# Weights times values of a grouped attention: two calls of four key tiles a head in place of four calls of two

## The chip, the cores and the metric

The kernel runs on one core of one Trainium2 chip. The metric is the device time of one execution in microseconds, and the comparison is between medians of several executions. The core's engines work side by side, each through its own list of instructions, and wait for each other through semaphores: TensorE (PE in the profile, its weight loads PEld), VectorE (DVE), ScalarE (ACT), GpSimd (POOL) and SyncE (SP). TensorE's clock has two levels, 2.4 GHz (granted clock 1.00) and 1.2 GHz (0.50).

## The reference

Two decoder layers over 1024 rows of 128 features: a selective scan, cross-attention, experts, causal attention, a cross-attention with state-space filter and feed-forward, and at the end a block of grouped attention and experts. Only the grouped attention matters here:

```python
NQ, NKV, HD = 16, 4, 8          # query heads, key/value heads, features of a head
q, k, v = ...                   # normalised and rotated, S rows each
k = jnp.repeat(k, NQ // NKV, axis=2)
v = jnp.repeat(v, NQ // NKV, axis=2)
scores = jnp.einsum('bthd,bshd->bhts', q, k) / np.sqrt(HD)
scores = jnp.where(causal[None, None], scores, -jnp.inf)
attn = jax.nn.softmax(scores, axis=-1)
out = jnp.einsum('bhts,bshd->bthd', attn, v)
```

## The kernel before

The program is a chain of parts with barriers between them; the grouped attention, `gqa_attend`, stands near its end, and `gqa_output` follows it. The kernel holds 1024 rows, so a head has NT = 8 query tiles and 8 key tiles of 128 (P); HALF is 512 rows. Queries and keys are split into three bfloat16 parts each.

For every one of the HQ = 16 heads five things are done:

- *Turn of the queries* (`turn`, L2623): eight transposes on TensorE, then ScalarE copies them out (qT, L2742).
- *Maxima* (L2638, L2641 on TensorE, L2722 on VectorE): for each query tile the scores of all keys up to the diagonal, with the causal mask added by a matmul, and the negated maximum of each row. Score banks are used in turn, so tile n needs that the maximum of tile n - 2 has been read.
- *Turn of the shifts* (L2623 again, 75 rows): VectorE splits the maxima into three parts (L2728 to L2731), TensorE transposes queries and maxima together, ScalarE copies them out (sT, L2752).
- *Exponentials* (L2651, L2654 on TensorE, L2759 on ScalarE): for key tile k the scores come out the other way round, keys in rows, with the maximum already subtracted; the exponential is written in float32 to `prob`. A key tile has one or two pieces of up to 512 columns, and a piece needs that the piece two before it has been read.
- *Weights times values* (`outputs`, L2670): the probabilities of a key tile times its values, 9 columns (8 features and a one for the sum). These matmuls use only a strip of 32 of TensorE's 128 columns, given by `tile_position`: even and odd key tiles and the two halves of the query rows have a strip each, four in all. All go to PSUM bank 7. A call works on a pair of key tiles: (0,1) and (2,3) have four matmuls each, (4,5) and (6,7) two, since their columns lie in the second half alone.

The order on each engine is written out by one loop over steps. Step 8h + i has the maxima of head h, tile i; the exponentials run 11 steps behind (EXP_LAG), the outputs 13 (OUT_LAG), the turn of the shifts 10 steps behind the head's first step, and the turn of the next head's queries comes at i = 5. So TensorE works on three heads at a time, and the calls of `outputs` for pairs (0,1), (2,3), (4,5), (6,7) stand at the ends of the steps with i = 6, 0, 2 and 4. When a head's last pair is done, VectorE copies and adds the two parts of its output (L2716, L2717) into `stack`, which `gqa_output` reads.

Of the kernel before, what the change touches and what calls it, by code (L numbers as in the profile page):

```python
# [23 lines left out]
P = 128  # L24
S = 1024
D = 128
NT = S // P
S2 = 6404
DC = 96
HALF = 512  # L30
# [90 lines left out]
def mamba(nc, g, t, m):  # L121
# [65 lines left out]
    N_LOADS = 13  # L187
    STEPS = NC * NS
    DT0 = BC3
# [2175 lines left out]
HQ, HKV, HD = 16, 4, 8  # L2365
# [199 lines left out]
def gqa_attend(nc, g, t, m, a):  # L2565
# [12 lines left out]
    prob = m.sb("prob", [P, 2, NT, S])  # L2578
# [26 lines left out]
    def out_quadrant(k, half):  # L2605
        q = 32 * (2 * (k % 2) + half)
        return ps[q:q + OUT, 7, :]
# [6 lines left out]

    Q_TURN, S_TURN, EXP_LAG, OUT_LAG = 5, NT + 2, NT + 3, NT + 5
    STEPS = HQ * NT + OUT_LAG

    with nc.Block() as block:
        @block.tensor
        def _(pe):  # L2620
            def turn(head, rows, done, bank=turned_bank):
                for i in range(NT):
                    last = pe.transpose(bank[0:rows, i * P:(i + 1) * P], split[:, i, head, 0:rows],  # L2623
                                        ident[:])
                last.then_inc(done, 1)

            def maxima(h, i):

                n = NT * h + i
                b = 2 * (n % 2)  # L2630
                if i == 0:
                    pe.wait_ge(q_ready, h + 1)
                if n >= 2:
                    pe.wait_ge(max_read, n - 1)
                width = (i + 1) * P
                for k in range(0, width, HALF):
                    w = min(HALF, width - k)
                    pe.matmul(ps[:, b + k // HALF, 0:w], qT[0:PARTS9, h % 2, i * P:(i + 1) * P],  # L2638
                              kT[0:PARTS9, h // (HQ // HKV), k:k + w], start=True, stop=k + w < width)
                col = (i % 4) * P  # L2640
                pe.matmul(ps[:, b + i // 4, col:col + P], ident[:], above[:], start=False,  # L2641
                          stop=True).then_inc(score_done, 1)

            def exponentials(h, k):

                if k == 0:
                    pe.wait_ge(s_ready, h + 1)
                for n, q, w in pieces(h, k):
                    if n >= 2:
                        pe.wait_ge(prob_ready, n - 1)  # L2650
                    last = pe.matmul(ps[:, 4 + n % 2, 0:w], kT[:, h // (HQ // HKV), k * P:(k + 1) * P],  # L2651
                                     sT[:, h % 2, k * P + q:k * P + q + w], start=True, stop=q > 0)
                    if q == 0:
                        last = pe.matmul(ps[:, 4 + n % 2, 0:P], ident[:], below[:], start=False, stop=True)  # L2654
                    last.then_inc(prob_psum, 1)

            def outputs(h, k):


                pe.wait_ge(prob_ready, pieces(h, k + 1)[-1][0] + 1)  # L2660
                if k == 0:
                    if h == 0:
                        pe.wait_ge(out_zeroed, 1)
                    else:
                        pe.wait_ge(o_ready, h)
                for half in range(2):
                    for kk in (k, k + 1):
                        lo, hi = max(kk * P, half * HALF), (half + 1) * HALF
                        if lo < hi:
                            last = pe.matmul(out_quadrant(kk, half)[:, lo - half * HALF:HALF],  # L2670
                                             a["v"][:, kk, h // (HQ // HKV), :],
                                             prob[:, h % 2, kk, lo - kk * P:hi - kk * P],
                                             start=kk < 2, stop=hi - (kk + 1) * P < 2 * P,
                                             tile_position=(0, 32 * (2 * (kk % 2) + half)))
                if k == NT - 2:
                    last.then_inc(pv_done, 1)

            for k in range(HKV):
                if k >= 2:
                    pe.wait_ge(k_ready, k - 1)  # L2680
                turn(HQ + k, SPLIT, k_psum, key_bank(k))
            pe.wait_ge(k_ready, HKV)
            turn(0, PARTS9, q_psum)
            for step in range(STEPS):
                h, k = divmod(step, NT)
                if k == Q_TURN and h + 1 < HQ:

                    pe.wait_ge(q_ready, 1) if h == 0 else pe.wait_ge(s_ready, h)
                    turn(h + 1, PARTS9, q_psum)
                h, k = divmod(step - S_TURN, NT)  # L2690
                if k == 0 and 0 <= h < HQ:
                    pe.wait_ge(q_ready, min(h + 2, HQ))
                    pe.wait_ge(shift_ready, h + 1)
                    turn(h, SPLIT, s_psum)
                h, k = divmod(step, NT)
                if h < HQ:
                    maxima(h, k)
                h, k = divmod(step - EXP_LAG, NT)
                if 0 <= h < HQ:
                    exponentials(h, k)  # L2700
                h, k = divmod(step - OUT_LAG, NT)
                if 0 <= h < HQ and k % 2:
                    outputs(h, k - 1)

        @block.vector
        def _(dve):
            link = chained(dve, chain_dve)
            dve.wait_ge(k_ready, HKV)
            dve.memset(ps[:, 7, :], 0.0).then_inc(out_zeroed, 1)
            for step in range(STEPS + 1):  # L2710
                h, k = divmod(step - OUT_LAG - NT, NT)
                if k == 0 and 0 <= h < HQ:

                    dve.wait_ge(pv_done, h + 1)
                    rows = a["stack"][64 * (h % 2):64 * (h % 2) + 64, h // 2, :]
                    link(dve.tensor_copy(rows, out_rows(0)))  # L2716
                    dve.tensor_tensor(rows, rows, out_rows(1), ALU.add).then_inc(o_ready, 1)  # L2717
                h, i = divmod(step, NT)
                if h < HQ:
                    b = h % 2  # L2720
                    dve.wait_ge(score_done, step + 1)
                    dve.tensor_reduce(low[:, b, i:i + 1], pair(2 * (step % 2), (i + 1) * P), AX, ALU.max,  # L2722
                                      negate=True).then_inc(max_read, 1)
                    if i == NT - 1:

                        dve.wait_ge(max_read, NT * (h + 1))
                        parts = split[:, :, h, PARTS9:SPLIT]
                        link(dve.tensor_copy(parts[:, :, 0], low[:, b, :]))  # L2728
                        link(dve.tensor_tensor(rest[:, b, :], low[:, b, :], parts[:, :, 0], ALU.subtract))
                        link(dve.tensor_copy(parts[:, :, 1], rest[:, b, :]))  # L2730
                        dve.tensor_tensor(parts[:, :, 2], rest[:, b, :], parts[:, :, 1],  # L2731
                                          ALU.subtract).then_inc(shift_ready, 1)

        @block.scalar
        def _(act):
            for k in range(HKV):
                act.wait_ge(k_psum, k + 1)
                act.activation(kT[:, k, :], key_bank(k), ACT.Copy).then_inc(k_ready, 1)

            def copy_queries(h):  # L2740
                act.wait_ge(q_psum, h + 1)
                act.activation(qT[0:PARTS9, h % 2, :], turned_bank[0:PARTS9, :], ACT.Copy).then_inc(q_ready, 1)  # L2742

            copy_queries(0)
            for step in range(STEPS):
                h, k = divmod(step, NT)
                if k == Q_TURN and h + 1 < HQ:
                    copy_queries(h + 1)
                h, k = divmod(step - S_TURN, NT)
                if k == 0 and 0 <= h < HQ:  # L2750
                    act.wait_ge(s_psum, h + 1)
                    act.activation(sT[:, h % 2, :], turned_bank, ACT.Copy).then_inc(s_ready, 1)  # L2752
                h, k = divmod(step - EXP_LAG, NT)
                if 0 <= h < HQ:
                    if h >= 2 and k == 0:
                        act.wait_ge(pv_done, h - 1)
                    for n, q, w in pieces(h, k):
                        act.wait_ge(prob_psum, n + 1)
                        act.activation(prob[:, h % 2, k, q:q + w], ps[:, 4 + n % 2, 0:w], ACT.Exp,  # L2759
                                       scale=SCALE).then_inc(prob_ready, 1)  # L2760
# [394 lines left out]
```

## Time and profile before

| | |
|---|---|
| median of 3 executions | 1744.25 us (1743.5 to 1744.35) |
| the profiled execution | 1739.54 us, its span 1737.8 us |
| TensorE (PE) busy | 1420.6 us, 82% |
| VectorE (DVE) busy | 1288.2 us, 74% |
| ScalarE (ACT) busy | 930.5 us, 54% |
| GpSimd (POOL) busy | 697.0 us, 40% |
| one head of the attention | 11.19 us |

The span is the time from the first instruction of the program to the last in the profile. Busy times are sums over all parts; what bounds one part has to be read in that part. The rows further down are of one profiled execution. A row that stands for several instructions in a run says so with "xN"; its time is from the start of the first to the end of the last. A float32 matmul leaves two records. The bracket behind a row is idle time of that engine and what ended it, as inferred from semaphores.

### The profile page before, as it was taken

The page shows a single profiled execution, that of the slowest core. Times are in us where ns is not written, and L with a number is a line of the kernel's source. Part 1 is how long each engine was busy: PE and PEld are TensorE (multiplying, and loading weights), DVE is VectorE, ACT ScalarE, POOL GpSimd, SP SyncE. Part 2 cuts the span into 40 slices and gives each one's busy share as a digit, 9 for nine tenths or more (in the row PEclk, how much of TensorE's full clock was granted, in tenths as well). Part 3 has the DMA queues.
Part 4 walks back from the last instruction along what each step waited for, and adds up shares of the span by engine and source line. Part 5 has one row for each costly group of instructions (what it writes and reads, how often), then busy time and mean ns, then how long its engine had stood idle before and what let it go on. Part 6 is the DMA issues. An engine that isn't in the chain of part 4 may idle for free. (4 is left out here: it accounts for less than half of the span.)

```text
span 1737.8 us, 19863 instructions
## 1 busy us (share of the span) xinstructions
PE 1420.6 (82%) x6581; PEld 752.1 (43%) x6637; DVE 1288.2 (74%) x3067; ACT 930.5 (54%) x1452; POOL 697.0 (40%) x529
## 2 busy tenths in 40 slices
PE   5777899899986747889898888988859339999798
PEld 2233344345544421355454554545547223333365
DVE  4998677855427539999999999999857666777433
ACT  4665212556521310788888888888831225666321
POOL 0664312012000000698898988989930030000012
PEclk9899899999987867999999999999888758999999
DMA  6000110000009320000000000000011030000000
GB/s 145 1 1 0 39 61 29 0 1 0 0 19 198 68 64 1 1 1 1 1 1 1 1 1 1 1 1 1 1 27 71 22 80 1 1 1 1 1 1 12
DMA packets 30968, 37.36 MB, mean 21 GB/s; under 512 B 13889, under 2 KB 24096, under 8 KB 29732
## 3 DMA queue, kind: packets, MB, share of 16 engines
q1 hardware_dynamic: 29312, 24.19, 5.1%
q10 hardware_dynamic: 1544, 11.79, 3.3%
q8 instruction: 56, 0.92, 0.2%
q14 instruction: 56, 0.46, 0.1%
HBM read 29.73 MB, written 6.24 MB: 21 GB/s over the span
## 5 line engine op out<-in xcount | busy, mean ns | idle before, releaser
L1461 PE MATMUL psum<-film_ka,film_context_qa 97*128 97x512 bf16 (+1 forms) x832 | 326.0, 393 | 86.8 <-DVE search_and_weigh_e L1695 36.5
L1665 DVE MAX8 search_and_weigh_kept<-psum 128x8 f32<-128x171 f32 (+2 forms) x1216 | 330.1, 324 | 0.2
L1463 PE MATMUL psum<-film_kb,film_context_qb 128*128 128x512 bf16 (+1 forms) x777 | 302.0, 390 | 0.0
L1847 ACT ACTIVATE search_and_weigh_e<-psum,search_and_weigh_bias 128x512 f32<-128x512 f32 (+1 forms) x416 | 267.5, 665 | 58.0 <-PE psum L1463 54.7
L1695 DVE SCALAR_TENSOR_TENSOR search_and_weigh_e<-psum,film_context_top,search_and_weigh_e 128x512 f32<-128x512 f32 (+1 forms) x283 | 200.0, 714 | 15.5 <-ACT search_and_weigh_e L1847 14.0
L1718 POOL TENSOR_TENSOR search_and_weigh_e<-search_and_weigh_e,search_and_weigh_keep 128x512 f32<-128x512 f32 (+1 forms) x133 | 150.6, 1132 | 108.6 <-ACT search_and_weigh_keep L1826 105.3
L1461 PEld LDWEIGHTS psum<-film_ka,film_context_qa 97*128 97x128 bf16 x832 | 86.3, 104 | 229.8 <-DVE search_and_weigh_e L1695 95.5
L1722 POOL TENSOR_TENSOR search_and_weigh_mean<-search_and_weigh_e 128x512 f32<-128x512 f32 (+1 forms) x104 | 133.4, 1283 | 11.5 <-DVE search_and_weigh_e L1695 4.4
L1752 PEld LDWEIGHTS psum<-ctx_rows,search_and_weigh_mean_T 128*128 128x128 f32 (+1 forms) x816 | 124.1, 195 | 31.3 <-issue 5.2
L2959 POOL TENSOR_TENSOR residual<-residual,top_expert_kept 128x1024 f32<-128x1024 f32 x7 | 16.5, 2355 | 292.2 <-DVE top_expert_kept L2916 292.2
L1727 POOL TENSOR_TENSOR search_and_weigh_mean<-search_and_weigh_mean,search_and_weigh_e 128x512 f32<-128x512 f32 (+1 forms) x104 | 127.9, 1230 | 8.2
L2722 DVE TENSOR_REDUCE gqa_attend_low<-psum 128x1 f32<-128x128 f32 (+7 forms) x128 | 94.0, 754 | 43.2 <-PE psum L2641 40.7
L1752 PE MATMUL psum<-ctx_rows,search_and_weigh_mean_T 128*128 128x96 f32 (+1 forms) x816 | 121.0, 271 | 1.0
L1726 POOL TENSOR_TENSOR search_and_weigh_e<-search_and_weigh_e 128x512 f32<-128x512 f32 (+1 forms) x91 | 111.8, 1229 | 7.1
L2759 ACT ACTIVATE gqa_attend_prob<-psum 128x512 f32<-128x512 f32 x192 | 84.9, 486 | 49.6 <-PE psum L2654 48.9
L1039 ACT ACTIVATE cross_attention_prob<-psum 128x1024 f32<-128x1024 f32 (+1 forms) x51 | 51.8, 1019 | 97.1 <-PE psum L998 96.4
L340 POOL TENSOR_TENSOR mamba_drive<-mamba_relu,mamba_b_all 128x1024 f32<-128x1024 f32 x32 | 77.2, 2414 | 64.7 <-ACT mamba_b_all L465 33.6
L985 PE MATMUL psum<-cross_attention_prob,ctx_rows 128*97 128x512 f32 (+1 forms) x204 | 98.2, 604 | 4.6 <-ACT cross_attention_prob L1039 4.6
L1825 ACT ACTIVATE search_and_weigh_keep<-search_and_weigh_e,search_and_weigh_below 128x512 bf16<-128x512 f32 (+1 forms) x133 | 93.5, 703 | 12.7 <-POOL search_and_weigh_mean L1727 12.2
L998 PE MATMUL psum<-oss_attention_qc_shifted,ctx_T 97*128 97x512 f32 (+1 forms) x204 | 99.3, 610 | 0.8 <-ACT oss_attention_qc_shifted L1030 0.8
L1463 PEld LDWEIGHTS psum<-film_kb,film_context_qb 128*128 128x128 bf16 x832 | 84.5, 102 | 33.4 <-issue 6.0
L1739 PE MATMUL psum<-ident,search_and_weigh_mean 128*128 128x128 f32 (+1 forms) x408 | 81.3, 281 | 11.7 <-ACT search_and_weigh_mean_T L1804 9.3
(544 smaller groups left out, 2660.1 us busy)
## 6 DMA issues: line engine op xcount, KB each, us to landing
film_kb<-film_k_rows ACTq DMA_DIRECT2D x4, 1601.0 KB
film_ka<-film_k_rows ACTq DMA_DIRECT2D x3, 1601.0 KB
ctx_T<-in_ctx_T SPq DMA_DIRECT2D x1, 2401.5 KB
gqa_experts_w<-in_L_ffn_W SPq DMA_DIRECT2D x1, 2048.0 KB
film_convolve_back<-in_dft_back SPq DMA_DIRECT2D x1, 1728.0 KB, 11.9
film_k_rows<-cross_attention_film_hi SPq DMA_DIRECT2D x6, 256.0 KB, 2.0
film_k_rows<-cross_attention_film_mid SPq DMA_DIRECT2D x6, 256.0 KB, 2.0
film_k_rows<-cross_attention_film_low SPq DMA_DIRECT2D x6, 256.0 KB, 2.0
```

Source lines behind the costliest of these rows:

```text
L985: last = pe.matmul(ps[0:CA, 6 + n, :], ctx[0:rows, k, :], prob[0:rows, k % 3, n * HALF:(n + 1) * HALF], start=k == 0, stop=k == KT - 1)
L998: last = pe.matmul(ps[0:rows, 2 * (k % 2) + n, :], ctx_T[:, k * P:k * P + rows], qc_shifted[:, n * HALF:(n + 1) * HALF], start=True, stop= ...
L1461: pe.matmul(out, a["qa"][0:ROWS, h, rows], a["ka"][0:ROWS, h, c + b:c + b + cols], start=True, stop=False)
L1463: last = pe.matmul(out, a["qb"][:, h, rows], a["kb"][:, h, c + b:c + b + cols], start=False, stop=True)
L1665: last = dve.max(kept[:, h % 2, first + s, :], bank[:, lo:hi])
L1695: dve.scalar_tensor_tensor(out=w, in0=weigh_bank(n, h), scalar=a["top"][:, NH * i + h, TOP - 1:TOP], in1=w, op0=ALU.is_ge, op1=ALU.mult).t ...
L1718: link(pool.tensor_tensor(w[h], w[h], keep[:, k % KEEPS, 0:width], ALU.mult))
L1722: link(pool.tensor_tensor(out, w[0], w[1], ALU.add))
L1726: link(pool.tensor_tensor(w[2], w[2], w[3], ALU.add))
L1727: pool.tensor_tensor(out, out, w[2], ALU.add).then_inc(mean_ready, 1)
L1752: last = pe.matmul(ps[:, 7, 0:DC], mean_T[0:r, n % 2, b:b + P], ctx[0:r, (c + b) // P, 0:DC], start=c + b == 0, stop=c + b + r == S2)
L1847: act.activation(e[:, n % RING, sub, 0:PIECES[u][1]], ps[:, SEARCH_BANKS + q % WEIGH_BANKS, 0:PIECES[u][1]], ACT.Exp, bias=bias[:, i % 2, ...
```

## The change

`outputs` works on four key tiles in a call (BURST = 4), and is called at every fourth key tile in place of every second. In a call the pairs follow each other in the order of before. It waits for the exponentials of its last key tile.

```diff
     STEPS = HQ * NT + OUT_LAG
+    BURST = 4
...
-                pe.wait_ge(prob_ready, pieces(h, k + 1)[-1][0] + 1)
+                pe.wait_ge(prob_ready, pieces(h, k + BURST - 1)[-1][0] + 1)
...
-                for half in range(2):
-                    for kk in (k, k + 1):
-                        lo, hi = max(kk * P, half * HALF), (half + 1) * HALF
-                        if lo < hi:
-                            last = pe.matmul(out_quadrant(kk, half)[:, lo - half * HALF:HALF],
...
-                if k == NT - 2:
+                for even in range(k, k + BURST, 2):
+                    for half in range(2):
+                        for kk in (even, even + 1):
+                            lo, hi = max(kk * P, half * HALF), (half + 1) * HALF
+                            if lo < hi:
+                                last = pe.matmul(out_quadrant(kk, half)[:, lo - half * HALF:HALF],
...
+                if k == NT - BURST:
                     last.then_inc(pv_done, 1)
...
-                if 0 <= h < HQ and k % 2:
-                    outputs(h, k - 1)
+                if 0 <= h < HQ and k % BURST == BURST - 1:
+                    outputs(h, k - BURST + 1)
```

The changed kernel's lines are numbered one higher from the maxima on (L2639 is the L2638 of before) and two higher in `outputs` (L2672 is L2670). A row names the line, the output and operands and the size of the result.

TensorE around exponentials 3 of a head, before: the call for pair (0,1) stands between the exponentials of key tile 3 and the next maxima.

```order
L2651 MATMUL psum<-gqa_attend_sT,gqa_attend_kT 128x512
L2654 MATMUL psum<-gqa_below,gqa_ident 128x128
L2651 MATMUL psum<-gqa_attend_sT,gqa_attend_kT 128x128
L2670 MATMUL psum<-gqa_attend_prob,gqa_v 9x512
L2670 MATMUL psum<-gqa_attend_prob,gqa_v 9x384
L2670 MATMUL psum<-gqa_attend_prob,gqa_v 9x512 x2
L2638 MATMUL psum<-gqa_attend_kT,gqa_attend_qT 128x512 x2
L2641 MATMUL psum<-gqa_above,gqa_ident 128x128
L2651 MATMUL psum<-gqa_attend_sT,gqa_attend_kT 128x512
L2654 MATMUL psum<-gqa_below,gqa_ident 128x128
```

The same place on TensorE in the changed kernel, from the last piece of exponentials 3 on:

```order
L2652 MATMUL psum<-gqa_attend_sT,gqa_attend_kT 128x128
L2639 MATMUL psum<-gqa_attend_kT,gqa_attend_qT 128x512 x2
L2642 MATMUL psum<-gqa_above,gqa_ident 128x128
L2652 MATMUL psum<-gqa_attend_sT,gqa_attend_kT 128x512
L2655 MATMUL psum<-gqa_below,gqa_ident 128x128
L2639 MATMUL psum<-gqa_attend_kT,gqa_attend_qT 128x128
L2642 MATMUL psum<-gqa_above,gqa_ident 128x128
L2652 MATMUL psum<-gqa_attend_sT,gqa_attend_kT 128x384
L2655 MATMUL psum<-gqa_below,gqa_ident 128x128
L2672 MATMUL psum<-gqa_attend_prob,gqa_v 9x512
L2672 MATMUL psum<-gqa_attend_prob,gqa_v 9x384
L2672 MATMUL psum<-gqa_attend_prob,gqa_v 9x512 x2
```

The pair (0,1) has moved behind the exponentials of key tiles 4 and 5, where it stands directly ahead of pair (2,3).

TensorE after the turn of the shifts, before: the call for pair (4,5) stands between exponentials 7 of one head and the maxima that precede exponentials 0 of the next.

```order
L2651 MATMUL psum<-gqa_attend_sT,gqa_attend_kT 128x128
L2654 MATMUL psum<-gqa_below,gqa_ident 128x128
L2670 MATMUL psum<-gqa_attend_prob,gqa_v 9x512
L2670 MATMUL psum<-gqa_attend_prob,gqa_v 9x384
L2638 MATMUL psum<-gqa_attend_kT,gqa_attend_qT 128x512
L2641 MATMUL psum<-gqa_above,gqa_ident 128x128
L2651 MATMUL psum<-gqa_attend_sT,gqa_attend_kT 128x512
L2654 MATMUL psum<-gqa_below,gqa_ident 128x128
```

The same place on TensorE in the changed kernel:

```order
L2652 MATMUL psum<-gqa_attend_sT,gqa_attend_kT 128x128
L2655 MATMUL psum<-gqa_below,gqa_ident 128x128
L2639 MATMUL psum<-gqa_attend_kT,gqa_attend_qT 128x512
L2642 MATMUL psum<-gqa_above,gqa_ident 128x128
L2652 MATMUL psum<-gqa_attend_sT,gqa_attend_kT 128x512
L2655 MATMUL psum<-gqa_below,gqa_ident 128x128
```

The pair (4,5) is gone from here, and stands directly ahead of pair (6,7), four steps after the merged call for tiles 0 to 3.

## Rows read from the trace of the kernel before

**Rows 1.** windows of one head and of the last stretch at low clock: busy us (xcount), granted clock

```profile
1491.15:1502.34 11.19, 10.31 (x82) 4.32 (x80) 7.87 (x15) 7.14 (x15) 0.00 (x0) 1.00 0.01 1
1446.00:1449.00 3.00, 3.00 (x15) 0.81 (x13) 1.52 (x2) 1.64 (x4) 0.00 (x0) 0.50 0.00 0
```

**Rows 2.** VectorE's second add for each head, L2717, of the whole trace

```profile
L2717 DVE TENSOR_TENSOR gqa_experts_stack<-gqa_experts_stack,psum x16: 689/691/693, 1457.6 to 1619.2; 64x512 f32<-64x512 f32 x16
```

**Rows 3.** waits of the attention: who waited, for whom, us, times, longest

```profile
PEld psum L2638 <- DVE gqa_attend_low L2722: 35.9, 42, 0.9
```

**Rows 4.** timeline of one head: start us, us, what, idle before and its releaser

```profile
1491.91 1.96 DVE L2722 TENSOR_REDUCE gqa_attend_low<-psum 128x1 f32<-128x768 f32 x2
...
1493.01 1.04 PE L2670 MATMUL psum<-gqa_attend_prob,gqa_v 128*9 128x512 f32 x8
1493.06 0.77 ACT L2759 ACTIVATE gqa_attend_prob<-psum 128x512 f32<-128x512 f32 x2 [0.27 <-PE psum L2654]
...
1493.99 0.61 PE L2638 MATMUL psum<-gqa_attend_kT,gqa_attend_qT 72*128 72x512 bf16 x2
...
1494.49 0.38 PE L2651 MATMUL psum<-gqa_attend_sT,gqa_attend_kT 75*128 75x512 bf16 x1
...
1495.05 0.22 PE L2654 MATMUL psum<-gqa_below,gqa_ident 128*128 128x128 bf16 x1
...
1495.20 1.05 PE L2670 MATMUL psum<-gqa_attend_prob,gqa_v 128*9 128x256 f32 x8
...
1496.18 0.28 PE L2638 MATMUL psum<-gqa_attend_kT,gqa_attend_qT 72*128 72x256 bf16 x1
...
1496.47 0.22 PE L2654 MATMUL psum<-gqa_below,gqa_ident 128*128 128x128 bf16 x1
...
1496.94 0.61 PE L2623 MATMUL psum<-gqa_ident,gqa_split 128*75 128x128 bf16 x8 [0.25 <-DVE gqa_split L2731]
...
1497.59 1.02 ACT L2752 ACTIVATE gqa_attend_sT<-psum 75x1024 bf16<-75x1024 bf16 x1 [0.48 <-PE psum L2623]
...
1497.82 1.02 PE L2670 MATMUL psum<-gqa_attend_prob,gqa_v 128*9 128x512 f32 x4
...
1498.78 0.39 PE L2638 MATMUL psum<-gqa_attend_kT,gqa_attend_qT 72*128 72x512 bf16 x1
...
1499.07 0.38 PE L2651 MATMUL psum<-gqa_attend_sT,gqa_attend_kT 75*128 75x512 bf16 x1
...
1501.01 0.60 PE L2670 MATMUL psum<-gqa_attend_prob,gqa_v 128*9 128x256 f32 x4
...
1501.54 0.64 PE L2623 MATMUL psum<-gqa_ident,gqa_split 128*72 128x128 bf16 x8
```

**Rows 5.** timeline of the last two gaps between heads

```profile
1603.85 3.30 DVE L2722 TENSOR_REDUCE gqa_attend_low<-psum 128x1 f32<-128x768 f32 x3
...
1608.18 0.61 PE L2623 MATMUL psum<-gqa_ident,gqa_split 128*75 128x128 bf16 x8 [0.54 <-DVE gqa_split L2731]
...
1608.83 1.02 ACT L2752 ACTIVATE gqa_attend_sT<-psum 75x1024 bf16<-75x1024 bf16 x1 [0.77 <-PE psum L2623]
...
1609.90 0.39 PE L2651 MATMUL psum<-gqa_attend_sT,gqa_attend_kT 75*128 75x512 bf16 x1
...
1614.00 0.77 ACT L2759 ACTIVATE gqa_attend_prob<-psum 128x512 f32<-128x512 f32 x2 [0.27 <-PE psum L2654]
...
1615.04 0.39 PE L2651 MATMUL psum<-gqa_attend_sT,gqa_attend_kT 75*128 75x512 bf16 x1
...
1616.61 0.28 PE L2651 MATMUL psum<-gqa_attend_sT,gqa_attend_kT 75*128 75x256 bf16 x1
...
1616.99 0.55 ACT L2759 ACTIVATE gqa_attend_prob<-psum 128x256 f32<-128x256 f32 x2 [0.49 <-PE psum L2654]
...
1617.00 1.46 PE L2670 MATMUL psum<-gqa_attend_prob,gqa_v 128*9 128x512 f32 x8
```

**Rows 6.** groups by form in the attention: xcount, busy us, mean ns, idle

```profile
L2759 ACT ACTIVATE gqa_attend_prob<-psum 128x512 f32<-128x512 f32 x93 | 53.7, 594 | 37.4 <-PE psum L2654 36.6
```

More of the change, by code:

```diff
@@ L2665, in outputs @@
                         pe.wait_ge(o_ready, h)
-                for half in range(2):
-                    for kk in (k, k + 1):
-                        lo, hi = max(kk * P, half * HALF), (half + 1) * HALF
-                        if lo < hi:
-                            last = pe.matmul(out_quadrant(kk, half)[:, lo - half * HALF:HALF],
[L2671 to L2674, printed above, removed]
-                if k == NT - 2:
+                for even in range(k, k + BURST, 2):
[4 more added lines that the diff above has]
+                                last = pe.matmul(out_quadrant(kk, half)[:, lo - half * HALF:HALF],
+                                                 a["v"][:, kk, h // (HQ // HKV), :],
+                                                 prob[:, h % 2, kk, lo - kk * P:hi - kk * P],
+                                                 start=kk < 2, stop=hi - (kk + 1) * P < 2 * P,
+                                                 tile_position=(0, 32 * (2 * (kk % 2) + half)))
+                if k == NT - BURST:
                     last.then_inc(pv_done, 1)
```

## The prediction, made before the changed kernel ran

> **What bounds the kernel now.** I first read the windows view, to see what kind of stretch the change sits in. A head of the grouped attention takes 11.19 us, in which TensorE is busy for 10.31 and the granted clock is 1.00, its upper level of 2.4 GHz; VectorE has 7.87 and ScalarE 7.14 [rows 1]. So this stretch goes by TensorE's own queue, and what counts there is how long TensorE stands. The sixteen second adds of L2717, one for each head, start from 1457.6 to 1619.2, 161.6 us [rows 2]: 13 gaps of 11.19, and the last two of 10.1 and 6.0 make the 16.1 that are left.
>
> The list of waits then has to be read with care. It puts 35.9 us on weight loads of L2638 that wait for VectorE's maxima of L2722 [rows 3]. In the timeline [rows 4] such a "wait" is the call of `outputs` itself. The row at 1493.01 is 8 matmul records (a float32 matmul leaves two) that lie beside each other in four column strips; the next score matmul starts at 1493.99. Its maximum (the first of the two from 1491.91, 1.96 us together) had been read by about 1492.9. So the call held the queue for 0.98 us and VectorE held nobody. What is to be seen is that the calls do two things. They take time, 0.98, 0.98, 0.96 and 0.53 us from their start to the next one's (1493.01, 1495.20, 1497.82, 1501.01). And they are filler: while they run, ScalarE and VectorE finish what TensorE needs next.
>
> **The price of a call's edges.** Back-to-back matmuls of 128 columns start 0.056 us apart (the turn at 1496.94: 8 in 0.61, of 0.22 each). Before the call at 1495.20 the step from 1495.05 is 0.15, so going in costs 0.15 - 0.06 = 0.09. Coming out: at the end of the attention the calls (4,5) and (6,7) already stand back to back, as one row of 1.46 us [rows 5]. By rows 4 a call holds the queue 0.06 less than its row is long (1.04 against 0.98), so this pair would hold it 1.40, where apart they hold it 0.96 + 0.53 = 1.49: 0.09 saved. Each merge thus saves 0.09 + 0.09 = 0.18, two a head: **-0.37 us**. The first merged call would then hold the queue 0.98 + 0.98 - 0.09 = 1.87 us; it is shown nowhere, and the nearest row is the second pair's. Its bounds are 1.82 (0.05 less, about as well as the edges can be read) and 1.96 (nothing saved on the way out). The Trainium skill, page "TensorEngine Tiling (Array Packing)", section "Tiling Modes", says that a switch of tiling mode drains TensorE; the trace agrees, with these 0.09 us on either side. By that rule alone the change could only gain, which is the first rival below.
>
> **What the moved calls uncover.** The matmuls are the same; pair (0,1) leaves the place after exponentials of key tile 3 and goes two steps on, and pair (4,5) leaves the place after exponentials of key tile 7 and goes two steps on. No semaphore is awaited later than before: the first call already waited for key tile 3 in its second half. TensorE's queue without its filler, place by place [rows 4]:
>
> - *After exponentials 3, place of (0,1).* The exponentials of key tile 4 need the score bank that ScalarE reads from 1493.06. A 128x512 exponential takes 0.594 [rows 6], and 0.05 passes from its end to TensorE's start (copy of sT, 1608.83 + 1.02, to 1609.90 [rows 5]): 1493.70. Without the call TensorE would be there at 1494.49 - 0.98 - 0.09 = 1493.42. **+0.28.** The score matmul between them, now at 1493.99, would come at 1492.92, when VectorE's maximum has only just ended (about 1492.9), so that one may wait some hundredths as well, inside this same wait.
> - *After exponentials 7, place of (4,5).* The first exponential of the next head (1499.07) needs sT, which ScalarE copies from 1497.59 for 1.02: ready at 1498.66. Without the call's 0.96 and its 0.09 TensorE would be there at 1498.02. **+0.64.** Now this wait is covered with 0.41 to spare.
> - *Before the turn of the shifts.* Here TensorE stands today: 1496.47 to 1496.94, less 0.06, is 0.41, for VectorE's four small operations (L2731). With the merged call ahead of it, TensorE comes 0.9 us later, and they are done: **-0.41.**
> - *Unchanged*: the two waits for exponentials before the call at 1501.01 and those after the copy of the queries, since no call is moved out of or into them.
>
> A head then costs +0.28 + 0.64 - 0.41 - 0.37 = **+0.14 us**, 13 gaps: **+1.8**.
>
> **The last two gaps** have no scores between, so less covers a call [rows 5]. In the gap of 10.1 the turn at 1608.18 waits for VectorE, whose three maxima run from 1603.85 for 3.30 whatever TensorE does, then the copy and exponential 0 at 1609.90 follow. So that chain stays, up to 0.2 earlier, and the last call grows from 0.53 to 1.40: +0.87 less up to 0.2, taken as **+0.75**. In the gap of 6.0, exponentials 4 (1615.04) lose the call (0,1): ScalarE started the one they wait for at 1614.00, ready at 1614.64, and TensorE would be there at 1615.04 - 1.07 = 1613.97: +0.67. There are now three separate calls, then two: -0.18. The last call must wait for exponential 7: ScalarE's two from 1616.99 for 0.55, and 0.05, is 1617.59, or 0.98 after exponentials 6 (1616.61), where (4,5) went in at 0.39 (1617.00): +0.59. Sum **+1.08**. Nothing follows that hides it: the heads' stack is the next stage's input.
>
> Until 1449 TensorE is at 1.2 GHz (0.50 [rows 1]); there its own work is longer and covers the waits, so the first merge gains a little: -0.1. Sum: 1.8 + 0.75 + 1.08 - 0.1 = **+3.5 us**. The profiled execution took 1739.54 us (span 1737.8), so 1743.0 in its terms; the timed median is 1744.25, 4.7 above it: 1744.25 + 3.5 = **1747.7 us**.
>
> **The rivals.**
>
> 1. *Faster: the filler isn't needed.* If the two uncovered waits weren't there, because ScalarE gets its work as much earlier as TensorE skips, the drains alone would count: 16 x 0.37 = 5.9 us less, **1738.3**. It speaks against it that sT can't be copied earlier relative to the turn, and the wait turns into a loss as soon as less than 1.05 - 0.41 = 0.64 us of filler stands between turn and exponential 0; all of it is moved away. That is the point from which it decides. 8%.
> 2. *No change.* The waits cost just what the drains give, and the end hides behind the drained stack: **1744.3**. For it: 0.51 against 0.37 are close, and an error of 0.1 in one wait closes the gap. Against it: the end's +1.8 doesn't hang on them. 9%.
> 3. *The clock rises later.* TensorE is still at 1.2 GHz between 1446 and 1449 [rows 1], in which the first call of `outputs` falls, and that call now comes up to 2.4 us later (twice the 1495.20 - 1493.99 = 1.21 us of scores that stand between the two places [rows 4]). The rise may then come later too. Three microseconds at half clock in which TensorE never stands (3.00 of 3.00 busy [rows 1]) cost half of them, 1.5 us more: **1749.2**. Against it: the scores that move up keep TensorE as busy. 15%.
> 4. *The merged call does not stream.* Four key tiles use each strip twice, and if the third's weights had to wait until the strip is empty, with a drain as at an edge, a merge would give nothing back: 16 x 0.37 = 5.9 us more, **1753.6**; half of it, 1750.6. The Trainium skill, page "TensorE: Matmul & The Clock Gate", section "Part 3: Packing small matmuls", says that weight loads overlap running matmuls only when the row group differs, and here it never does; the trace speaks against it, since the pair of 1.46 us [rows 5] shows both calls in less time than apart. 8%.
> 5. *As forecast*, 60%: from +2.6 (13 x 0.07 less, by a first merged call of 1.82 and waits 0.02 shorter) to +4.9 (16 x 0.09 more, by one of 1.96): **1746.8 to 1749.2**.
>
> **How the numbers follow.** What a measurement of this kernel can tell from no change is about 0.2%, 3.5 us; my forecast lies on that edge, so the forecast case splits, 30 within and 30 above. Slower: 30, 14 of rival 3 and 7 of rival 4, together 51%. Within: 30, the 9 of rival 2, and 1 each of rivals 3 and 4, together 41%. Faster: the 8% of rival 1. The range, 1743.5 to 1751.0, takes in the forecast case, rivals 2 and 3 and half of rival 4; rival 1 and the full rival 4 are left out.
>
> **What would show it.** In the profile after: two rows of `outputs` a head, near 1.9 and 1.46 us; a head's gap of 11.3 us in place of 11.19; no idle time of TensorE before the turn; a wait of about 0.6 for the copy L2752 (2753 there) before exponential 0, and one of 0.3 before exponentials 4; a last gap of 7.1 us in place of 6.0. If the gap is under 11.19 the two waits are wrong, and if the first call is over 2.0 us long rival 4 is right. A clock of 0.50 beyond 1449 would be rival 3. VectorE's maxima (L2722) becoming what TensorE waits for would be something that I have priced at hundredths only.

## The result, and the profile after

The changed kernel is slower: 1748.8 us (median of 6, 1748.4 to 1750.83) against 1742.88 us (median of 6, 1739.35 to 1744.35). The ratio is 1.0036, with a 95% interval of 1.0024 to 1.0048, so 0.36% or some 5.9 us. The profiled execution took 1748.59 us (span 1746.8), 9.05 more than that of before. The forecast was 1747.7 us, +3.5. It lies 1.1 us from the measured time only because it was added to a median of before, 1744.25, that six executions put at 1742.88; as a difference it is 2.4 us too small.

First the row of VectorE's second add, whose line is now L2719, for the first fourteen heads. It is the pace of the heads that [rows 2] gave before.

```profile
L2719 DVE TENSOR_TENSOR gqa_experts_stack<-gqa_experts_stack,psum x14: 690/691/693, 1461.4 to 1608.8; 64x512 f32<-64x512 f32 x14
```

Thirteen gaps in 147.4 us are 11.34 us each; the forecast was 11.33, and before they were 11.19. Next, from the windows view of the kernel after: one head, two stretches of the last head, and the end of the low clock at the start of the stage. The columns are those of [rows 1].

```profile
1494.70:1506.04 11.34, 10.09 (x83) 4.75 (x82) 7.79 (x15) 7.15 (x14) 0.00 (x0) 1.00 0.01 1
1618.60:1622.00 3.40, 2.19 (x17) 0.91 (x20) 1.37 (x2) 2.20 (x6) 0.00 (x0) 1.00 0.00 0
1622.00:1625.40 3.40, 3.40 (x20) 0.86 (x11) 0.00 (x0) 0.57 (x3) 0.00 (x0) 0.50 0.00 0
1451.00:1454.70 3.70, 3.70 (x22) 1.19 (x20) 2.08 (x6) 1.09 (x2) 0.00 (x0) 0.50 0.00 0
1455.00:1458.00 3.00, 2.50 (x25) 1.55 (x24) 1.58 (x3) 1.84 (x4) 0.00 (x0) 1.00 0.00 0
```

In a head TensorE is busy for 10.09 us, 0.22 less than in [rows 1], and stands for 1.25 where it stood for 0.88: the busy time shrank and the idle time grew by more. (A busy time counts the last matmul before a wait at its full 0.22 us, where in a row of matmuls the next starts after 0.06; so each wait is about 0.16 us longer than the idle time that stands in a bracket.) The lower rows hold what the forecast did not have. The clock is at 0.50 until 1454.7, where before it had risen by 1449 (2.3 of these 5.7 us are a later start of the stage, as shown below), and near the end of the attention, from 1622.0 to 1625.4, it is at 0.50 again, where before it stayed at 1.00.

The timeline of one head of the kernel after, TensorE's calls and what stands around them, beside [rows 4]:

```profile
1497.57 0.22 PE L2642 MATMUL psum<-gqa_above,gqa_ident 128*128 128x128 bf16 x1
1497.92 0.39 PE L2652 MATMUL psum<-gqa_attend_sT,gqa_attend_kT 75*128 75x512 bf16 x1
...
1498.64 1.91 PE L2672 MATMUL psum<-gqa_attend_prob,gqa_v 128*9 128x512 f32 x16
...
1500.48 0.28 PE L2639 MATMUL psum<-gqa_attend_kT,gqa_attend_qT 72*128 72x256 bf16 x1
...
1500.77 0.22 PE L2655 MATMUL psum<-gqa_below,gqa_ident 128*128 128x128 bf16 x1
...
1500.83 0.61 PE L2624 MATMUL psum<-gqa_ident,gqa_split 128*75 128x128 bf16 x8
...
1501.83 0.22 PE L2642 MATMUL psum<-gqa_above,gqa_ident 128*128 128x128 bf16 x1
...
1502.55 0.39 PE L2652 MATMUL psum<-gqa_attend_sT,gqa_attend_kT 75*128 75x512 bf16 x1 [0.50 <-ACT gqa_attend_sT L2754]
...
1504.50 1.46 PE L2672 MATMUL psum<-gqa_attend_prob,gqa_v 128*9 128x512 f32 x8
...
1505.89 0.64 PE L2624 MATMUL psum<-gqa_ident,gqa_split 128*72 128x128 bf16 x8
```

Each step of the forecast is there. The first merged call holds the queue from 1498.64 to 1500.48, 1.84 us (forecast 1.87), the second from 1504.50 to 1505.89, 1.39 (forecast 1.40). Exponentials 4 start at 1497.92, where the step from 1497.57 would be 0.06: a wait of 0.29. The turn at 1500.83 follows 0.06 behind its neighbour: its wait of 0.41 is gone. Exponentials 0 start at 1502.55, 0.72 behind the score matmul of 1501.83: a wait of 0.66 for the copy of sT. That copy is now waited for once in each head but the first; the waits view of before has one such wait in all. Only the waits for exponentials, which stood there before too, are larger (waits view of the kernel after, 1455 to 1622):

```profile
PEld psum L2652 <- ACT gqa_attend_prob L2761: 30.6, 74, 0.9
PEld psum L2652 <- ACT gqa_attend_sT L2754: 12.8, 15, 1.2
PEld psum L2639 <- DVE gqa_attend_low L2724: 11.8, 14, 0.9
PE psum L2652 <- ACT gqa_attend_sT L2754: 7.9, 15, 1.0
```

The third row is what is left of the 35.9 us of [rows 3]. About two thirds of that "wait" vanished with the calls that stood there, as it was never one: TensorE was busy with them.

The last head in the timeline of the kernel after, beside [rows 5]:

```profile
1619.52 0.69 DVE L2719 TENSOR_TENSOR gqa_experts_stack<-gqa_experts_stack,psum 64x512 f32<-64x512 f32 x1
...
1620.95 0.39 PE L2652 MATMUL psum<-gqa_attend_sT,gqa_attend_kT 75*128 75x512 bf16 x1 [0.63 <-ACT gqa_attend_prob L2761]
...
1621.56 3.22 PE L2672 MATMUL psum<-gqa_attend_prob,gqa_v 128*9 128x512 f32 x16
...
1624.71 0.39 PE L2652 MATMUL psum<-gqa_attend_sT,gqa_attend_kT 75*128 75x256 bf16 x1
...
1625.25 0.55 ACT L2761 ACTIVATE gqa_attend_prob<-psum 128x256 f32<-128x256 f32 x2 [2.83 <-PE psum L2655]
1625.85 1.46 PE L2672 MATMUL psum<-gqa_attend_prob,gqa_v 128*9 128x512 f32 x8 [0.43 <-ACT gqa_attend_prob L2761]
...
1628.08 0.69 DVE L2719 TENSOR_TENSOR gqa_experts_stack<-gqa_experts_stack,psum 64x512 f32<-64x512 f32 x1
```

The call that takes 1.91 us in every other head takes 3.22 here, in the stretch at 0.50, and the gap from add to add is 8.56 us where 7.1 was forecast.

**The sum of the profiles.** The stage starts with the first score matmul. Its row of before (L2638) and of the kernel after (L2639):

```profile
L2638 PE MATMUL psum<-gqa_attend_kT,gqa_attend_qT x192: 217/379/635, 1429.8 to 1605.5; 72*128 72x512 bf16 x96, 72*128 72x128 bf16 x32, 72*128 72x256 bf16 x32, 72*128 72x384 bf16 x32
```

```profile
L2639 PE MATMUL psum<-gqa_attend_kT,gqa_attend_qT x192: 216/379/634, 1432.1 to 1610.7; 72*128 72x512 bf16 x96, 72*128 72x128 bf16 x32, 72*128 72x256 bf16 x32, 72*128 72x384 bf16 x32
```

So 2.3 of the 9 us lie ahead of the stage, in code that the change does not touch. Within it: from that start to the first add 29.3 us in place of 27.8, **+1.5**; thirteen gaps of 11.34 in place of 11.19, **+1.9**; the gap of 10.1 is 10.74, **+0.65**; the gap of 6.0 is 8.56, **+2.55**; together **+6.6**, and some 0.2 behind it.

### The profile page after: what moved, and what is told of

Read it like the earlier page. It is cut to its first block and busy times, and to the rows that moved or that the text cites. A ratio compares the mean times of both kernels' runs of the same rounds, so it can differ in the third digit from the quotient of the medians.

```text
span 1746.8 us, 19863 instructions
## 1 busy us (share of the span) xinstructions
PE 1416.0 (81%) x6581; PEld 757.5 (43%) x6637; DVE 1289.8 (74%) x3067; ACT 931.6 (53%) x1452; POOL 697.0 (40%) x529
## 5 line engine op out<-in xcount | busy, mean ns | idle before, releaser
L1463 PE MATMUL psum<-film_kb,film_context_qb 128*128 128x512 bf16 (+1 forms) x777 | 298.0, 384 | 0.0
L924 DVE TENSOR_REDUCE cross_attention_tops<-psum 128x1 f32<-128x1024 f32 (+1 forms) x56 | 61.4, 1109 | 36.1 <-PE psum L968 36.0
```

The costliest lines, as they stand in the source:

```text
L1463: last = pe.matmul(out, a["qb"][:, h, rows], a["kb"][:, h, c + b:c + b + cols], start=False, stop=True)
```

## The experiments

All kernels take the changed kernel and give `outputs` a number of key tiles; a table says when it is called. An entry is (first key tile, tiles in the call, step counted from the head's first, whether ahead of that step's exponentials). Before is `((0, 2, 14, False), (2, 2, 16, False), (4, 2, 18, False), (6, 2, 20, False))`, the change `((0, 4, 16, False), (4, 4, 20, False))`. No computation is left out in any of them. "First add" is the time from the first score matmul to the first add, 27.8 us before and 29.3 after. Ratios are to the kernel before on the same chip, with 95% intervals.

**e1: only the first two calls merged.**

```diff
-    BURST = 4
+    def CALLS(h):
+        return ((0, 4, 16, False), (4, 2, 18, False), (6, 2, 20, False))
...
-            def outputs(h, k):
+            def outputs(h, k, count):
...
-                for even in range(k, k + BURST, 2):
+                for even in range(k, k + count, 2):
...
+            def calls(step, early):
+                for h in range(HQ):
+                    for k, count, after, before_exps in CALLS(h):
+                        if step == h * NT + after and before_exps == early:
+                            outputs(h, k, count)
...
+                calls(step, True)
                 if 0 <= h < HQ:
                     exponentials(h, k)
...
-                if 0 <= h < HQ and k % BURST == BURST - 1:
-                    outputs(h, k - BURST + 1)
+                calls(step, False)
```

> Only pairs (0,1) and (2,3) are one call, in the place of (2,3); (4,5) and (6,7) stay where they were. My theory (edges 0.18 us a merge, and what each moved call uncovers): +0.28 for exponentials 4, -0.41 because the turn of the shifts no longer waits, -0.18 for the edges, so a gap of 11.19 - 0.31 = 10.88 us and some 4 us less in all (about 0.2%), minus or plus 1.5 for when the clock rises. Rival (a longer call is slower in itself, the drain theory turned round): a gap over 11.2 us. Rival (only drains count): 11.01 us.

**e2: only the last two calls merged.**

```diff
+        return ((0, 2, 14, False), (2, 2, 16, False), (4, 4, 20, False))
```

> Only pairs (4,5) and (6,7) are one call, in the place of (6,7). My theory: +0.64 for the wait for the copy of sT, -0.18 for the edges, and the turn still waits its 0.41: a gap of 11.65 us, 13 of them +6.0, the last two gaps +0.9 and +0.6, in all +7.5 us (0.43%). If only drains counted: 11.01 us and faster. If merging itself cost the loss of the change: half of it, a gap of 11.27.

**e3: the first call moved, but not merged.** It goes ahead of exponentials 5, two steps later than before, and scores stand between it and the call for (2,3).

```diff
+        return ((0, 2, 16, True), (2, 2, 16, False), (4, 2, 18, False), (6, 2, 20, False))
```

> As the kernel in which only (0,1) and (2,3) are merged, but the two stay apart: (0,1) stands one group of exponentials ahead of (2,3), so the cover is nearly the same and one pair of edges comes back. My theory: its gap plus 0.18 to 0.20, that is 11.06 us. If a merge saved nothing: the same gap as the merged one. If a merged call streams worse: a shorter gap than the merged one.

Measured: e1 1741.98 us against 1743.4, ratio 0.9986 (0.9972 to 1.0); e2 1752.93, ratio 1.0049 (1.0033 to 1.0066); e3 1742.67, ratio 0.9992 (0.9977 to 1.0006). The row of the second add for the first fourteen heads, of e1, e2 and e3 in turn:

```profile
L2726 DVE TENSOR_TENSOR gqa_experts_stack<-gqa_experts_stack,psum x14: 690/691/691, 1462.1 to 1603.5; 64x512 f32<-64x512 f32 x14
```

```profile
L2726 DVE TENSOR_TENSOR gqa_experts_stack<-gqa_experts_stack,psum x14: 690/691/691, 1462.8 to 1614.3; 64x512 f32<-64x512 f32 x14
```

```profile
L2726 DVE TENSOR_TENSOR gqa_experts_stack<-gqa_experts_stack,psum x14: 689/691/692, 1462.5 to 1606.8; 64x512 f32<-64x512 f32 x14
```

One head takes 10.88, 11.66 and 11.10 us (a thirteenth of 141.4, 151.6 and 144.3; in hundredths e2's row runs from 1462.77 to 1614.35). The forecast's terms give 11.19 + 0.28 - 0.41 - 0.18 = 10.88, 11.19 + 0.64 - 0.18 = 11.65 and 11.19 + 0.28 - 0.41 = 11.06. So the terms hold one by one: the first merge gains 0.32 a head, the second loses 0.46, and the change is their sum. The difference of e3 and e1 is the price of the first merge's edges, 0.22 where 0.18 was read from the timeline; the wait before exponentials 4 is 0.29 in both. For the second merge e2 leaves about 0.2: the wait of 0.66 less the 0.46 that was lost. That e1's 4 us over thirteen heads are hardly there in its time has two places in its profile: the first add comes after 29.5 us, and its last gap is 9.27, with the clock low again from 1613.9 to 1620.7. (Its profiled execution, 1743.9 us, is one of its slower ones; they run from 1735.34 to 1744.36.) e2 took 9.5 us more than before where 7.5 were expected. In its profile the first add comes after 28.8 us, and the gap of 10.1 is 12.17, with the clock low from 1621.9 to 1625.4; its last gap, 6.61, is as expected. So e1 and e2 are confirmed in the heads and were missed at the start and in the tail.

**e4: the change, but the last two heads called as before.**

```diff
+        if h < HQ - 2:
+            return ((0, 4, 16, False), (4, 4, 20, False))
+        return ((0, 2, 14, False), (2, 2, 16, False), (4, 2, 18, False), (6, 2, 20, False))
```

> The changed kernel for heads 0 to 13, and the four calls of before for heads 14 and 15. My theory: gaps of 11.34 us as in the changed kernel, the last two 10.1 and 6.0 us as before, and no fall of the granted clock among the exponentials of the last head; in all 3.2 us less than the changed kernel. If the fall of the clock near the end has nothing to do with the last heads' calls, it comes all the same and the last gap stays over 7 us.

Measured: 1746.55 us against 1743.4, ratio 1.0014 (1.0002 to 1.0026). Heads stay at 11.34; the last two gaps are back at 10.10 and 6.01, and the clock does not fall in them. The windows view of e4, the middle of its last gap:

```profile
1614.00:1617.40 3.40, 2.79 (x15) 0.64 (x12) 0.04 (x1) 2.91 (x6) 0.00 (x0) 1.00 0.00 0
```

**e6: the change, with a tail that leaves TensorE no pauses.** Fourteen score matmuls of 512 columns are put where TensorE waits in the last head. They write a bank that nobody reads any more, and their result is not used.

```diff
+            def keep_busy(step):
+                h, k = divmod(step - EXP_LAG, NT)
+                if h == HQ - 1:
+                    for _ in range({0: 4, 1: 2, 3: 3, 4: 3}.get(k, 0)):
+                        pe.matmul(ps[:, 0, :], qT[0:PARTS9, 0, 0:P], kT[0:PARTS9, 0, 0:HALF],
+                                  start=True, stop=True)
+                if step == STEPS - 1:
+                    for _ in range(2):
+                        pe.matmul(ps[:, 0, :], qT[0:PARTS9, 0, 0:P], kT[0:PARTS9, 0, 0:HALF],
+                                  start=True, stop=True)
```

> The changed kernel, with 14 more score matmuls of 512 columns (results unused) where TensorE waits in the last head: 4, 2, 3 and 3 ahead of exponentials 0, 1, 3 and 4, and 2 ahead of the last call. My theory: the clock fell among the last exponentials because TensorE stands too much there; kept busy it stays at 1.00, and the last gap is 7.1 us in place of 8.56, although there is more work. Rival (the last gap is long from the call's own waits): it stays at 8.5 or gets longer by the added work of 3 us.

Measured: 1746.34 us against 1742.69, ratio 1.0018 (1.0004 to 1.0033). The windows view of e6 and then its timeline, the last head:

```profile
1616.50:1619.90 3.40, 3.40 (x21) 1.21 (x17) 1.37 (x2) 1.74 (x5) 0.00 (x0) 1.00 0.00 0
```

```profile
1617.88 0.69 DVE L2738 TENSOR_TENSOR gqa_experts_stack<-gqa_experts_stack,psum 64x512 f32<-64x512 f32 x1
...
1619.91 1.91 PE L2674 MATMUL psum<-gqa_attend_prob,gqa_v 128*9 128x512 f32 x16
...
1624.96 0.69 DVE L2738 TENSOR_TENSOR gqa_experts_stack<-gqa_experts_stack,psum 64x512 f32<-64x512 f32 x1
```

With more work in it the last gap is shorter: 7.08 us in place of 8.56. The call takes 1.91 again. The stretch ahead of it is now busy throughout (3.40 of 3.40, where the kernel after had 2.19), and the clock stays at 1.00. And 7.08 is what the forecast's waits give at full clock (6.01 + 1.08 = 7.09). This splits the +2.55: 1.07 of waits, 1.48 of clock. The split rests on this profile; e6's median is too near the changed kernel's to confirm 1.5 us (ratios 1.0018 against 1.0036 and, measured again, 1.0043, with intervals that overlap), and its first add came 0.8 us earlier than the changed kernel's, which its edit does not explain.

**e7: e1, but the last two heads as before.**

```diff
+        if h < HQ - 2:
+            return ((0, 4, 16, False), (4, 2, 18, False), (6, 2, 20, False))
+        return ((0, 2, 14, False), (2, 2, 16, False), (4, 2, 18, False), (6, 2, 20, False))
```

> (0,1) and (2,3) merged in heads 0 to 13, four calls as before in heads 14 and 15. My theory: 13 gaps of 10.88 us less what the switch back costs, the last two 10.1 and 6.0, the clock stays up, in all 4.0 us less than before, minus or plus 1.5 for the rise. The gap in which it switches back has one more pair of edges.

Measured: 1740.37 us against 1742.69, ratio 0.9988 (0.9977 to 0.9998). Heads of 10.88, last gaps of 10.10 and 6.01, first add after 29.0. The time is 2.3 us less than before, where 4.0 were expected, plus or minus 1.5 for the rise; the first add comes 1.2 us later than before's. The best of the merged forms gains 0.12%, within what this kernel's measurement can tell from no change.

**e5: no merge; the two outer calls one place earlier**, ahead of the exponentials of their step. So (0,1) stands ahead of exponentials 3 and (6,7) ahead of exponentials 1 of the next head, where TensorE waited for ScalarE before.

```diff
+        return ((0, 2, 14, True), (2, 2, 16, False), (4, 2, 18, False), (6, 2, 20, True))
```

> Four calls of two key tiles as before, but (0,1) stands ahead of exponentials 3 and (6,7) ahead of exponentials 1, where TensorE waits 0.55 and 0.30 + 0.21 us for ScalarE. My theory says that where a call stands is what counts, not how many there are: a gap of about 10.1 us, the last two 9.1 and 7.2, some 14 us less in all. If ScalarE or the edges of the calls set the pace, the gap stays near 11.2. The first call is as early as before or earlier, so if the place of the first call sets when the clock rises, it rises about 19 us after the first score matmul as before, not 23 as in the changed kernel.

Measured: 1725.46 us against 1742.69, ratio 0.9914 (0.9898 to 0.9929). In the timeline of e5, with the lines of TensorE about the two moved calls, and then in its windows view, two heads:

```profile
1494.98 0.22 PE L2644 MATMUL psum<-gqa_above,gqa_ident 128*128 128x128 bf16 x1
1495.13 0.60 PE L2674 MATMUL psum<-gqa_attend_prob,gqa_v 128*9 128x256 f32 x4
1495.66 0.39 PE L2654 MATMUL psum<-gqa_attend_sT,gqa_attend_kT 75*128 75x512 bf16 x1
...
1497.71 0.22 PE L2644 MATMUL psum<-gqa_above,gqa_ident 128*128 128x128 bf16 x1
1497.86 1.04 PE L2674 MATMUL psum<-gqa_attend_prob,gqa_v 128*9 128x512 f32 x8
1498.84 0.39 PE L2654 MATMUL psum<-gqa_attend_sT,gqa_attend_kT 75*128 75x512 bf16 x1
```

```profile
1496.60:1516.68 20.08, 19.80 (x164) 8.63 (x162) 15.65 (x29) 14.06 (x29) 0.00 (x0) 1.00 0.00 1
```

A head takes 10.05 us on the mean (10.17 and 9.92 in turn), and TensorE stands for 0.14 of it, where it stood for 0.88. All eight edges a head are still paid. The busy time fell from 10.31 to 9.90 us with the same matmuls, as each wait that goes takes some 0.16 us of it along (an estimate from the steps of 0.22 and 0.06 above). Over thirteen heads that is 15 us, where some 14 were expected for the whole kernel; the medians differ by 17.2 and the profiles' spans by 14.9.

**e8: e5, but the last head as before.**

```diff
+        if h < HQ - 1:
+            return ((0, 2, 14, True), (2, 2, 16, False), (4, 2, 18, False), (6, 2, 20, True))
+        return ((0, 2, 14, False), (2, 2, 16, False), (4, 2, 18, False), (6, 2, 20, False))
```

> As the kernel with calls ahead of the waits, but the last head as before. My theory: 13 gaps of 10.1 us; the last head's calls fall into its own waits as before, so that the clock stays up and the last gap is 6 to 7 us. If the clock falls at the end of the other kernel (gap over 8), this one is the faster by 1 to 2 us.

Measured: 1725.04 us against 1742.69, ratio 0.9903 (0.9883 to 0.9923). The last gap is 7.12 in place of e5's 7.27, the heads are the same. There was nothing to win in the tail, as e5's clock had not fallen there.

**e9: the change, but the first head called as before. e10: before, but the first head called as in the change.** They ask whether the later place of the first call is what delays the rise of the clock.

```diff
+        if h > 0:
+            return ((0, 4, 16, False), (4, 4, 20, False))
+        return ((0, 2, 14, False), (2, 2, 16, False), (4, 2, 18, False), (6, 2, 20, False))
```

> The changed kernel, with the four calls of before for head 0. So far the clock rose 19.2 to 20.7 us after the first score matmul where the first call stood behind exponentials 3 or ahead of them (three profiles), and 21.2 to 24.3 us after it where it stood behind exponentials 5 (six profiles). My theory: the place of the first call decides, so 19 to 21 us here, and some 1 us less in all than the changed kernel. Rival (chance in the phase of what measures the activity): anything from 19 to 24.

```diff
+        if h == 0:
+            return ((0, 4, 16, False), (4, 4, 20, False))
+        return ((0, 2, 14, False), (2, 2, 16, False), (4, 2, 18, False), (6, 2, 20, False))
```

> The kernel before, with the two calls of the changed one for head 0 alone. My theory: the clock rises 22 to 24 us after the first score matmul, the first add comes 29 us after it in place of 27.8, the rest is as before: gaps of 11.19 us, 10.1 and 6.0, some 1.5 us more in all. Rival (chance): anything from 19 to 24.

**changed_again: the changed kernel once more**, for a second profile.

> The changed kernel once more. Gaps of 11.34, 10.74 and over 8 us if the fall of the clock near the end is its rule, 7.1 us if it was chance; the rise 22 to 24 us after the first score matmul. Time as first measured: 0.2% to 0.5% over the kernel before.

Measured: e9 1750.7 us against 1741.63, ratio 1.0048 (1.0033 to 1.0063); e10 1744.15, ratio 1.0015 (1.0001 to 1.0028); changed_again 1748.26, ratio 1.0043 (1.0028 to 1.0059). The first add of e9 comes after 28.3 us, 1.0 earlier than in the changed kernel; that of e10 after 28.85, 1.1 later than before. Both go the expected way. But e9 as a whole did not get faster, a miss: its clock was low in the tail for longer, and its last two gaps were 11.50 and 9.97, with the same calls there as in the changed kernel. The windows view of e9:

```profile
1617.10:1627.30 10.20, 8.71 (x39) 2.40 (x36) 1.37 (x2) 3.30 (x9) 0.00 (x0) 0.50 0.00 0
```

The windows view of changed_again shows the picture of the kernel after a second time, the same 3.40 us at 0.50 behind the same 2.19 us busy; its last gap is 8.55. Its first score matmul starts at 1429.7, as before's, so the 2.3 us ahead of the stage are not the change's.

```profile
1616.30:1619.70 3.40, 2.19 (x19) 0.95 (x22) 1.37 (x2) 2.23 (x6) 0.00 (x0) 1.00 0.00 0
1619.70:1623.10 3.40, 3.38 (x20) 0.81 (x11) 0.00 (x0) 0.58 (x3) 0.00 (x0) 0.50 0.00 0
```

That equal start also gives the fairest comparison of the rise. The windows view of before and then of changed_again, the 3.30 us from 1449.1 on:

```profile
1449.10:1452.40 3.30, 3.05 (x28) 1.25 (x26) 2.30 (x7) 1.36 (x3) 0.00 (x0) 1.00 0.00 0
```

```profile
1449.10:1452.40 3.30, 3.30 (x20) 0.84 (x18) 1.61 (x6) 1.09 (x2) 0.00 (x0) 0.50 0.00 0
```

Their clocks rise at 1449.0 and 1452.4, and their first adds come after 27.8 and 29.3 us. e5 and e8, which start at 1429.5 and 1429.8 too and call early, rise at 1448.8 and 1449.1. TensorE was busy for all of the 3.00 us from 1446 in before and in changed_again alike, so its busy time does not tell why the one rose and the other did not.

A thin stretch is not always followed by a fall. In the kernel after, TensorE was busy for still less of 3.40 us earlier in the tail, and in e3 for 2.15 in the last gap; the clock stayed at 1.00 in both and in the 3 us behind them. The windows view of the kernel after and then of e3:

```profile
1613.60:1617.00 3.40, 1.86 (x17) 0.89 (x15) 0.00 (x0) 2.65 (x5) 0.00 (x0) 1.00 0.00 0
```

```profile
1615.02:1618.42 3.40, 2.15 (x14) 0.72 (x13) 1.37 (x2) 2.78 (x7) 0.00 (x0) 1.00 0.00 0
```

## Why the forecast had the direction and missed part of the size

- **The head, +0.14: right.** Measured +0.145, and e1, e2 and e3 confirm its terms in three combinations, within 0.01, 0.01 and 0.04 us. Small errors cancelled: the edges are worth 0.22 in the first merge and about 0.2 in the second, not 0.18, and the waits came out at 0.29 and 0.66 in place of 0.28 and 0.64.
- **The gap of 10.1, +0.75: right** to a tenth (0.65).
- **The gap of 6.0, +1.08: the mis-sized term**, with 2.55 measured. "Nothing follows that hides it" was worked out at full clock. The waits that the term counts are right (e6: +1.07), but the clock fell for 3.4 us in the last head, and that is the other 1.48. That it belongs to the waits of the last two heads is supported from two sides: take them away (e4, and e7 against e1) or fill them (e6), and the fall is gone, while the changed calls in the tail were profiled three times (after, changed_again, e9) and had it each time. The medians agree for e4: its interval, up to 1.0026, ends below that of changed_again, from 1.0028. In profiles, the clock fell in the tail of the changed kernel (both times), e1, e2 and e9, and in none of before, e3, e4, e5, e6, e7, e8 and e10. Each but the changed kernel is one profile. When the clock falls and for how long (3.4 us in the changed kernel, 10.2 in e9 with the same calls there), and why it passed the thinner stretch of 1.86 us busy, stays open.
- **The start, -0.1: wrong sign, +1.5 measured.** That is rival 3, given 15% and priced at 1.5. That the place of the call matters is borne out where the stages start alike (before, e5 and e8 against changed_again: a rise 3.4 us later, a first add 1.5 us later); how large its effect is elsewhere is not settled. The clock rose 19.2 to 21.0 us after the first score matmul in the five profiles whose first head is called early (before, e2, e5, e8, e9), and 21.2 to 24.3 us after it in the eight in which it is late. The two groups do not overlap, but nearly touch, and e9 and e10 move the first add by 1.0 and 1.1 and not by 1.5. Their stages start 2.5 to 2.7 us later than before's, so they are not a like comparison, and each is one execution. By what the place of the call delays the rise is not shown.
- Sum: 3.5 + 1.6 for the start + 1.5 for the last gap - 0.1 = 6.5, beside 6.6 in the profiles and 5.9 in the medians. e4, which takes the tail's part away, has +3.15 in its medians and +3.5 in its profile's stage.
- **Rivals.** *Faster, the filler isn't needed*: refuted by the waits of 0.29 and 0.66, and turned round by e5, where the same filler in the right places takes 17 us. *No change*: refuted, the interval begins at 1.0024. *The merged call does not stream*: refuted, it holds the queue 1.84 us, less than two calls of 0.98. By the rule that was cited there, of the Trainium skill's page "TensorE: Matmul & The Clock Gate", section "Part 3: Packing small matmuls", the third and fourth tiles' weight loads should have waited; the trace does not agree.

## What to carry to other kernels

On an in-order queue an independent piece of work is worth what it covers: its two edges cost 0.2 us here, its place up to 0.66 us a head. Before merging such pieces, list the waits that each covers, and look for waits that none covers; merging saved 0.4 us of edges and 0.4 of a wait a head and uncovered 0.95 elsewhere, while moving two calls in front of waits took 1.1 us off each head with no merge at all (ratio 0.9914). And price a drained tail at both levels of the clock, since pauses there can come with a fall of it.

## What was not expected of the hardware

- The clock fell in the last head with no long pause before it. In the 3.4 us ahead TensorE was busy for 2.19, and its longest idle time was 0.63 us; then followed 3.4 us at 0.50 (1.2 GHz), in which the merged call took 3.22 us in place of 1.91. Two profiles of the same kernel agree on it. Yet a stretch with 1.86 us busy, 5 us earlier, was passed at 1.00.
- Adding work shortened the time: with fourteen unused matmuls in the last head its gap was 1.5 us shorter (e6), in one profile.
- The clock can stay low under full load: at 0.50 TensorE was busy 3.70 of the last 3.70 us before the rise at 1454.7, and in changed_again for all of 1446.0 to 1449.0 and of 1449.1 to 1452.4.
- In e5 the gaps alternate between 10.17 and 9.92 us, all thirteen of them, though the program of each is the same. Why was not looked into.
